# One program for self-attention and the first cross-attention of a decoder layer, with two pairs of sequences projected early

## The chip, the cores and the metric

The kernel runs on one core of a Trainium2 chip. The metric is the device time of one execution in microseconds (us). Engines: PE (TensorE) multiplies matrices into eight banks of PSUM, DVE (VectorE), ACT (ScalarE) and POOL (GpSimd) work elementwise, and SP (SyncE) issues transfers. Each engine takes its instructions in the order written and waits at semaphores.

## The reference

A decoder of two layers works on `x` of 16 sequences of 128 tokens with 256 features, in float32. The change concerns two of its six sublayers:

```python
x = x + _L0_attn_ref(_layernorm(x, axis=-1), ...)
x = x + _L0_xattn_ref(_layernorm(x, axis=-1), ctx_1024, ctx_1024, L0_xattn_W_q, L0_xattn_b_q, ...)
```

`_L0_attn_ref` is five state-space layers and then causal self-attention with 16 heads of 64, its output projection and a layer norm. `_L0_xattn_ref` is attention with 16 heads of 16 over a context of 128 tokens per sequence: Q from the normed `x`, K and V from the context, each with a bias, softmax over 128 keys, an output projection with a bias. A mixture of experts, a second self-attention, a second cross-attention and a quantized product follow; their code is unchanged.

## The kernel before

The kernel is a chain of stages. Each stage writes one program per engine inside an `nc.Block()`; all engines meet at the end of a block, and after a stage one more block clears the stage's semaphores on POOL (`clear_semaphores`).

**Self-attention** (`stage_self_attention`, L539) works in 64 ticks, `m` = 0 to 63, and ends with 8 ticks of tail, up to `LAST_TICK` = 72. The work is cut into 8 halves: 4 groups of 4 sequences, and in each two octets of heads. A tick handles 4 heads of one sequence, and two ticks make a unit (one sequence, one octet). At tick `m`, PE computes scores (L646, at even `m`), turns the probabilities of tick `m-3` (L657), multiplies those of tick `m-5` and its neighbour with V (L674) and makes the output product of tick `m-8`'s unit (L44 to L46, 12 matmuls), DVE adds the mask (L750) and takes maxima (L753), ACT takes exponentials (L707), POOL multiplies by the inverse sums (L810). The q, k and v of the next half are made by 12 "jobs" in the ticks of this half; in the last half (ticks 56 to 63) there are none. DVE adds a unit's output to `act` (octet 0) or `a_res` (octet 1) at L776, which counts up `y_added`. The layer norm follows for octet 1, and POOL adds into `x_res` (L801), which counts up `x_ready`.

**Cross-attention** (`stage_cross_attention`, L883) goes over 8 pairs of sequences for the projections and 16 sequences for attention. A pair `n` has the steps `project_k` (PE L1082), `copy_k` (four operations on DVE, L1001), `project_v` (L1091), `copy_v` (L1030), `measure` and `norm` of `x`, `turn_z` (L1099), `copy_z` (DVE L1006), `project_q` (L1107), `copy_q` (DVE L1015). They share one bank, `JOB`, so these steps of one pair, and of the next, follow one another. A sequence has `scores` (L1120, four banks `S[0..3]`, of which there is one set), `maxima` (DVE L1036, four banks), `exps` (ACT L1064, four banks of four), `invert_sums` (DVE L1040), `share_out` (POOL L962), `turn_probs` (PE L1131), `copy_probs` (ACT L1068 for banks 0, 1, 3 and DVE L921 for bank 2), `outputs` (PE L1144), `copy_out`, `project_o` (L1153) and `add`. Scores of a sequence wait for all exps of the one before. `measure_next` takes the statistics for the expert stage. The order on each engine comes from a table of places: a pair's step stands at its number plus 104 for each pair, a sequence's at its number plus 52 for each sequence, and each engine sorts its steps by place:

```python
BEAT = 52
"project_k": 91, "project_v": 117, "copy_v": 127, "measure": 14, ...
"scores": (172,), "maxima": (182, 184, 214, 200), "exps": (212, 213, 220, 218), ...
DVE_COPIES = (2,)
```

SP and ACT issue the loads at the start of the stage: the first context pair, the four weights, the biases, and then the experts' weights, one expert (1.5 MB) for each later pair (L2256). `decoder` calls the stages.

Of the kernel before, what the change touches and what calls it, by code (L numbers as in the profile page):

```python
# [12 lines left out]
F32 = mybir.dt.float32  # L13
# [4 lines left out]
ALU = mybir.AluOpType  # L18
# [520 lines left out]
def stage_self_attention(nc, ctx, io, mem):  # L539
# [15 lines left out]
    q_t = sb("q_t", [P, KW, GT])  # L555
    k_t = sb("k_t", [P, KW, GT])
    v = sb("v", [P, GS, WIDE])
# [7 lines left out]
    zb = sb("zb", [P, D])  # L565
    stats, mv, ve = mem["stats"], mem["mv"], mem["ve"]
# [43 lines left out]
    with nc.Block() as block:  # L610
        @block.tensor
        def _(pe):
            def job(half, j):
                n = half * JOBS + j
                G, octet = divmod(half, 2)
                if n >= 2:
                    pe.wait_ge((job_act, job_dve)[j % 2], n // 2)
                bank = JOB[j % 2]
                if j < 2 * OCT:
                    weights, c = (wq, wk)[j % 2], octet * OCT + j // 2  # L620
                    for k in range(KD):
                        mm = product(pe, bank[:, :], [x[:, k, c * P:(c + 1) * P] for x in weights], [x[:, k, G * GT:(G + 1) * GT] for x in ACT_T],
                                     k == 0, k == KD - 1)
                else:
                    t = G * GT + (j - 2 * OCT) * P
                    for k in range(KD):
                        mm = product(pe, bank[:, :], [x[:, k, t:t + P] for x in ACT_T],
                                     [x[:, k, octet * BANK:(octet + 1) * BANK] for x in wv], k == 0, k == KD - 1)
                mm.then_inc(job_ready, 1)

            pe.wait_ge(mem["attn_w_split"], 16)
            for j in range(JOBS):
                job(0, j)
            for m in range(LAST_TICK + 1):
                if m < TICKS and m % 2 == 0:
                    G, octet, s, _ = place(m)
                    if m % HALF_TICKS == 0:
                        jobs = (m // HALF_TICKS) * (JOBS // 2) + OCT
                        pe.wait_ge(job_act, jobs)
                        pe.wait_ge(job_dve, jobs)  # L640
                    if m >= 2:
                        pe.wait_ge(masked, m)
                    for i in range(4):
                        for par in range(2):
                            rows = slice(par * HEAD, (par + 1) * HEAD)
                            mm = pe.matmul(S[par][:, i * P:(i + 1) * P], q_t[rows, OCT * octet + i, s * P:(s + 1) * P],  # L646
                                           k_t[rows, OCT * octet + i, s * P:(s + 1) * P], start=True, stop=True,
                                           tile_position=(par * HEAD, 0))
                            if i == 3:
                                mm.then_inc(s_ready, 1)  # L650
                t = m - TURN
                if 0 <= t < TICKS:
                    pe.wait_ge(prob_ready, t + 1)
                    if t >= 2:
                        pe.wait_ge((pt_dve, pt_act)[t % 2], t // 2)
                    for i in range(4):
                        tr = pe.transpose(PT[t % 2][:, i * P:(i + 1) * P], prob[:, t % 4, i, :], ident[:, :])  # L657
                    tr.then_inc(pt_ready, 1)
                t = m - MEAN
                if 0 <= t < TICKS and t % 2 == 1:  # L660
                    G, octet, s, _ = place(t)
                    U = t // 2
                    if t % HALF_TICKS == 1:
                        jobs = (t // HALF_TICKS + 1) * (JOBS // 2)
                        pe.wait_ge(job_act, jobs)
                        pe.wait_ge(job_dve, jobs)
                    if U >= 2:
                        pe.wait_ge(y_added, U - 1)
                    pe.wait_ge(pt_dve, U + 1)
                    pe.wait_ge(pt_act, U + 1)  # L670
                    for i in range(4):
                        for par in range(2):
                            head = octet * 8 + 2 * i + par
                            mm = pe.matmul(OT(U)[par * HEAD:(par + 1) * HEAD, i * P:(i + 1) * P],  # L674
                                           v[:, s, head * HEAD:(head + 1) * HEAD], prob_t[:, (t - 1 + par) % 4, i, :],
                                           start=True, stop=True, tile_position=(0, par * HEAD))
                    mm.then_inc(ot_ready, 1)
                unit = behind(m, OUT)
                if unit:
                    U, G, octet, s = unit  # L680
                    pe.wait_ge(ot_hi, U + 1)
# [5 lines left out]
                for half, j in jobs_at(m):  # L687
                    job(half, j)
# [1630 lines left out]
```

## Time and profile before

| | us |
|---|---|
| Median of 3 runs (lowest, highest) | 1304.44 (1303.21, 1308.12) |
| Profiled execution, its own time | 1305.01 |
| Its span, first to last instruction | 1303.2 |
| PE busy / DVE busy / ACT busy / POOL busy | 1142.3 / 836.0 / 646.5 / 663.5 |
| Mean granted TensorE clock | 0.946 of full |
| First exponentials of self-attention, first scores of cross-attention, first instruction of the expert stage | 417.4, 741.3, 893.3 |

In a timeline a row gives the start, the length, the engine, the line, the operation, its output and input and how many instructions are merged; in brackets is how long the engine had been idle before and what ended that. The granted clock has two levels, 0.50 (1.2 GHz) and 1.00 (2.4 GHz), and a stretch shows their mean.

### The profile page before, as it was taken

Reading aid. Unit: us, or ns where it says so; the run is one execution under the profiler, and the core shown is the slowest. Engines: PE = TensorE matmul, PEld = TensorE weight load, DVE = VectorE, ACT = ScalarE, POOL = GpSimd, SP = SyncE. Lnnn points to the kernel's source line nnn. Section 1 sums busy time; section 2 is a strip of 40 time slices with the busy share of each in tenths; the row PEclk is TensorE's granted clock in tenths of the full one; section 3 lists DMA queues with packets and bytes.
Section 4 is the critical chain, followed back from the end, with each engine's and each line's share of the span. In section 5 each row is a group of like instructions: output and inputs, shape, how many; then the busy total and the mean of one; then the engine's idle time right before and its main releaser. Section 6 shows DMA issues by size and latency. Waiting matters only on the chain. (4 is left out here: it accounts for less than half of the span.)

```text
span 1303.2 us, 21174 instructions
## 1 busy us (share of the span) xinstructions
PE 1142.3 (88%) x6835; PEld 891.9 (68%) x6835; DVE 836.0 (64%) x1886; ACT 646.5 (50%) x1892; POOL 663.5 (51%) x706
## 2 busy tenths in 40 slices
PE   4999999999978999999975599985499999995984
PEld 3788888888866887887864477765266666664862
DVE  6888889888872666666664388873543333323795
ACT  2555555555533555555553188882122444224873
POOL 3276767767561224233344377762156656552664
PEclk9999999999998999999989599997599999997995
DMA  4002010010000000000000433204332323222001
GB/s 154 11 1 77 2 37 39 16 60 16 17 1 1 2 1 1 1 1 1 1 1 1 161 115 114 107 2 138 97 75 42 49 41 48 42 37 70 1 18 49
DMA packets 38078, 53.73 MB, mean 41 GB/s; under 512 B 8320, under 2 KB 32896, under 8 KB 36448
## 3 DMA queue, kind: packets, MB, share of 16 engines
q1 hardware_dynamic: 28672, 41.50, 9.4%
q0 software_dynamic: 8736, 10.25, 5.1%
q8 instruction: 52, 0.85, 0.3%
q10 hardware_dynamic: 576, 0.79, 0.2%
q14 instruction: 42, 0.34, 0.1%
HBM read 40.78 MB, written 11.74 MB: 40 GB/s over the span
## 5 line engine op out<-in xcount | busy, mean ns | idle before, releaser
L414 DVE SCALAR_TENSOR_TENSOR ssm_conv<-bank,conv_w,ssm_conv 128x508 f32<-128x508 f32 (+2 forms) x240 | 159.2, 727 | 9.6 <-ACT ssm_conv L350 9.6
L707 ACT ACTIVATE a_prob<-a_prob,a_neg_max 128x128 f32<-128x128 f32 x256 | 99.7, 391 | 121.3 <-DVE a_neg_max L753 121.0
L1407 PE MATMUL bank<-expert_raw,e_rows_t 128*128 x312 | 148.9, 601 | 1.2 <-ACT e_rows_t L1494 1.2
L303 PE MATMUL bank<-w_out,ssm_u 128*128 128x256 f32 x640 | 143.5, 382 | 0.0
L303 PEld LDWEIGHTS bank<-w_out,ssm_u 128*128 128x128 f32 x640 | 119.9, 190 | 17.9
L810 POOL TENSOR_TENSOR a_prob<-a_prob,a_inv 128x512 f32<-128x512 f32 x64 | 66.2, 1040 | 125.4 <-DVE a_inv L758 125.4
L1064 ACT ACTIVATE x_prob<-bank,x_neg_max 128x128 f32<-128x128 f32 x256 | 89.6, 400 | 39.1 <-DVE x_neg_max L1036 39.1
L1334 POOL DMA_INDIRECT x_rows<-e_y,e_index x39 | 62.9, 1612 | 75.8 <-ACT e_y L1522 72.0
L508 POOL TENSOR_TENSOR act_t_lo<-ssm_turned,act_t_hi 128x512 fp32r<-128x512 f32 x40 | 51.6, 1289 | 97.9 <-ACT ssm_turned L375 97.9
L1660 DVE COPY e_h_t<-bank 128x512 f32<-128x512 f32 x39 | 26.9, 691 | 105.0 <-PE bank L1416 105.0
L962 POOL TENSOR_TENSOR x_prob<-x_prob,x_inv 128x512 f32<-128x512 f32 x64 | 66.0, 1040 | 48.7 <-DVE x_inv L1040 48.7
L1407 PEld LDWEIGHTS bank<-expert_raw,e_rows_t 128*128 128x128 f32 x312 | 56.9, 193 | 42.9 <-issue 41.0
L44 PE MATMUL bank<-act_t_hi,w_in_hi 128*128 128x512 f32 x200 | 80.7, 403 | 2.5 <-PEq L66 1.7
L350 ACT ACTIVATE ssm_conv<-bank,conv_b,conv_w 128x512 f32<-128x512 f32 x80 | 62.0, 779 | 36.7 <-PE bank L46 35.6
L45 PE MATMUL bank<-act_t_lo,w_in_hi 128*128 128x512 f32 x200 | 78.9, 394 | 0.0
L46 PE MATMUL bank<-act_t_hi,w_in_lo 128*128 128x512 f32 x200 | 78.6, 393 | 0.0
L450 DVE TENSOR_SCALAR ssm_res<-ssm_res,mv,ve 128x256 f32<-128x256 f32 x80 | 71.0, 928 | 6.8 <-POOL ve L475 5.4
L1424 PE MATMUL bank<-expert_raw,e_h_t 128*128 x312 | 73.9, 380 | 0.9 <-DVE e_h_t L1660 0.9
L359 ACT ACTIVATE ssm_u<-ssm_conv 128x512 f32<-128x512 f32 x80 | 47.6, 635 | 48.5 <-DVE ssm_conv L414 48.3
L1318 POOL DMA_INDIRECT e_rows<-z_rows,e_index x39 | 38.7, 993 | 46.6 <-DVE e_index L1641 35.1
L1064 ACT ACTIVATION_READ_ACCUMULATOR x_prob<-bank,x_neg_max 128x1 f32 x256 | 61.8, 241 | 0.0
L1424 PEld LDWEIGHTS bank<-expert_raw,e_h_t 128*128 128x128 f32 x312 | 56.3, 190 | 7.6 <-issue 1.6
(328 smaller groups left out, 2997.4 us busy)
## 6 DMA issues: line engine op xcount, KB each, us to landing
expert_raw<-in_experts_laid SPq DMA_DIRECT2D x8, 1536.0 KB, 8.1
attn_raw<-in_attn_w_laid SPq DMA_DIRECT2D x4, 1024.0 KB, 7.4
w_in_raw<-in_L_attn_in_proj_w SPq DMA_DIRECT2D x5, 640.0 KB, 8.4
w_out<-in_L_attn_out_proj_w SPq DMA_DIRECT2D x5, 512.0 KB, 3.9
x_res<-in_x SPq DMA_DIRECT2D x4, 512.0 KB, 5.7
x_context<-in_ctx_t_laid SPq DMA_DIRECT2D x8, 256.0 KB, 3.6
z_rows<-cv SPq DMA_DIRECT2D x4, 512.0 KB, 2.9
x_rows<-x_res SPq DMA_DIRECT2D x4, 512.0 KB, 4.6
```

The lines of the kernel that those rows point to most:

```text
L44: pe.matmul(out, lhs[HI], rhs[HI], start=start, stop=False)
L45: pe.matmul(out, lhs[HI], rhs[LO], start=False, stop=False)
L46: return pe.matmul(out, lhs[LO], rhs[HI], start=False, stop=stop)
L303: mm = pe.matmul(UWY[h][:, s * D:(s + 1) * D], u[:, g % 2, c, t:t + P], w_out[:, c, :], start=(c == 0), stop=(c == KI - 1))
L414: op = dve.scalar_tensor_tensor(out=acc, in0=xs, scalar=conv_w[:, c, TAPS - 1 - back:TAPS - back], in1=acc, op0=ALU.mult, op1=ALU.add)
L450: dve.tensor_scalar(res[:, h, s, :], res[:, h, s, :], mv[:, i, 0:1], ve[:, i:i + 1], ALU.subtract, ALU.mult).then_inc(z_ready, 1)
L707: e = act.activation(prob[:, m % 4, i, :], prob[:, m % 4, i, :], ACT.Exp, bias=neg_max[:, m % 4, i:i + 1], accum_out=total[:, m % 4, i:i + 1])
L810: pool.tensor_tensor(prob[:, t % 4, :, :], prob[:, t % 4, :, :], inv[:, t % 4, :].unsqueeze(2).broadcast_to([P, 4, P]), ALU.mult).then_inc ...
L962: pool.tensor_tensor(prob[:, n % 2, r, :, :], prob[:, n % 2, r, :, :], inv[:, n % 2, r, :].unsqueeze(2).broadcast_to([P, 4, P]), ALU.mult) ...
L1064: e = act.activation(prob[:, n % 2, r, i, :], S[r][:, i * P:(i + 1) * P], ACT.Exp, bias=neg_max[:, n % 2, r, i:i + 1], accum_out=total[:, ...
L1407: mm = pe.matmul(bank[:, :], rows_t[:, t % 2, k, :], W[:, bass.ds(at + (column + k * FFN), FFN)], start=(k == 0), stop=(k == KD - 1))
L1424: mm = pe.matmul(Y, h_t[:, t % 2, f, :], W[:, bass.ds(at + (DOWN_AT + f * D), D)], start=(f == 0), stop=(f == KF - 1))
```

## The change

1. The two stages become functions that emit steps, and `decoder` writes one block for both. The block between them that cleared semaphores is gone. POOL clears self-attention's semaphores at the step `invert` of the last pair.
2. The projections of pairs 0 and 1 (`EARLY = 2`) are written into self-attention's ticks 56 to 64, each at the end of its tick, and use bank 2 (a bank of the jobs). From tick 72 on, cross-attention follows in each engine's program without a barrier.
3. The loads of cross-attention's weights and context start on SP once `y_added` has reached 24, those of the last weight and the experts later.
4. `copy_z`, `copy_q` and half of `copy_k` (the odd heads, now `copy_k_odd`) go from DVE to ACT; the copy of the probabilities' bank 3 goes from ACT to DVE. Every place in the table is new.
5. Cross-attention's tiles lie in memory that self-attention has finished with: weights and context over `act`, the projections' tiles over the turned activations, the experts' weights over those of self-attention.

```diff
 BY_PAIR = {
-    "project_k": 91, "project_v": 117, "copy_v": 127, "measure": 14, "invert": 0, "norm": 47, "turn_z": 135, "copy_z": 147,
+    "project_k": 75, "project_v": 115, "copy_v": 102, "measure": 0, "invert": 86, "norm": 98, "turn_z": 136, "copy_z": 127,
...
-DVE_COPIES = (2,)
+DVE_COPIES = (2, 3,)
+EARLY = 2
+EARLY_TICKS = {"clear_v": (56, 56), "selections": (57, None), "measure": (56, 59), "invert": (56, 59), "norm": (57, 60), "project_k": (57, 61), "copy_k": (57, 61),
+               "copy_k_odd": (57, 61), "project_v": (58, 62), "copy_v": (58, 62), "turn_z": (59, 63), "copy_z": (59, 63),
+               "project_q": (60, 64), "copy_q": (60, 64)}
+LEAD = {72: 0}
...
-    S, PT_BANK, JOB = psum[0:4], psum[4:6], psum[6]
+    S, PT_BANK = psum[0:4], psum[4:6]
+    job_bank = lambda n: psum[2] if n < EARLY else psum[6]
...
+        sp.wait_ge(attention["y_added"], 3 * SEQS // 2)
+        load(0, "W_k")
             load_context(0)
...
+            if G == 3:
+                sp.wait_ge(attention["x_ready"], SEQS)
+                sp.dma_start(w_o[:, :], io["L0_xattn_W_o_laid"]).then_inc(w_loaded[3], 16)
+            if G >= 3:
+                mem["load_expert"](sp, G - 3)
...
+                if n == PAIRS - 1:
+                    for handle in attention["handles"]:
+                        pool.sem_clear(handle)
...
+            elif phase == "copy_k_odd":
+                act.wait_ge(k_even, n + 1)
+                for k in range(KD):
+                    kc = act.activation(k_t[:, n % 2, 1, k, :], job_bank(n)[:, k * PT:(k + 1) * PT], ACT.Identity, bias=bk_odd[:, k:k + 1],
+                                        scale=sel[:, 1:2])
...
+            elif phase == "copy_q":
+                act.wait_ge(q_ready, n + 1)
+                    qc = act.activation(q_t[:, n % 2, k, :], job_bank(n)[:, k * PT:(k + 1) * PT], ACT.Identity, bias=bq_scaled[:, k:k + 1],
+                                        scale=XHEAD ** -0.5)
...
                 if phase == "project_k":
+                elif n == EARLY:
+                    pe.wait_ge(attention["y_added"], 2 * SEQS - 1)
...
+                @block.tensor
+                def _(pe):
+                    attention["tensor"](pe, cross["following"]("tensor"))
+                    cross["rest"]("tensor", pe)
```

DVE's order in the middle of the changed cross-attention, from the `maxima` of sequence 4 (`x_neg_max`) on. `stats` and `mv` are `measure_next`, `x_stats` is `measure`, `x_prob_t` the copies of banks 2 and 3, `x_v` is `copy_v`:

```order
750 L1061 TENSOR_REDUCE x_neg_max<-bank 128x4
751 L1017 BN_STATS stats<-x_res 128x6 x2
752 L1020 BN_AGGR mv<-stats 128x2 x2
753 L1022 TENSOR_SCALAR ve<-mv 128x2
754 L1061 TENSOR_REDUCE x_neg_max<-bank 128x4 x2
755 L1072 TENSOR_TENSOR x_res<-bank,x_res 128x256
756 L1065 RECIPROCAL x_inv<-x_total 128x4
757 L946 COPY x_prob_t<-bank 128x512 x2
758 L1065 RECIPROCAL x_inv<-x_total 128x4
759 L1055 TENSOR_TENSOR x_v<-bank,x_bv 128x16x16 x2
760 L1061 TENSOR_REDUCE x_neg_max<-bank 128x4
761 L1017 BN_STATS x_stats<-x_res 128x6 x2
```

Before, `measure_next` stood ahead of the first maximum, one copy of probabilities stood between the second and the third, and `copy_k` in place of `copy_v`.

ACT's order over two sequences of the changed cross-attention, an even one first: `x_prob` are exponentials, four to a bank, `x_z_t`, `x_q_t` and `x_k_t` the moved copies:

```order
388 L1109 ACTIVATE x_prob_t<-bank 128x512
389 L1097 ACTIVATE x_z_t<-bank 128x512
390 L1109 ACTIVATE x_prob_t<-bank 128x512
391 L1084 ACTIVATE x_prob,x_total<-bank,x_neg_max 128x128 x4
392 L1105 ACTIVATE x_q_t<-bank,x_columns 128x256 x2
393 L1084 ACTIVATE x_prob,x_total<-bank,x_neg_max 128x128 x12
394 L1109 ACTIVATE x_prob_t<-bank 128x512
395 L1092 ACTIVATE x_k_t<-bank,x_columns 128x256 x2
396 L1109 ACTIVATE x_prob_t<-bank 128x512
397 L1084 ACTIVATE x_prob,x_total<-bank,x_neg_max 128x128 x16
```

Before, the order was 16 exponentials and three copies of probabilities for each sequence, and nothing else.

DVE's order in self-attention's ticks 57 and 58 after the change. `a_` names are self-attention's, the `x_` rows are new:

```order
645 L748 TENSOR_TENSOR a_prob<-bank,causal 128x512
646 L751 TENSOR_REDUCE a_neg_max<-a_prob 128x4
647 L756 RECIPROCAL a_inv<-a_total 128x4
648 L760 COPY a_prob_t<-bank 128x512
649 L765 TENSOR_TENSOR a_o_t_lo<-bank,a_o_t_hi 128x512
650 L1027 TENSOR_REDUCE x_columns<-ident 128x2
651 L1030 TENSOR_SCALAR x_columns<-x_columns 128x2
652 L1031 TENSOR_SCALAR x_columns<-x_columns 128x2
653 L1040 TENSOR_SCALAR x_k_t<-bank,x_columns 128x256 x2
654 L748 TENSOR_TENSOR a_prob<-bank,causal 128x512
655 L751 TENSOR_REDUCE a_neg_max<-a_prob 128x4
656 L756 RECIPROCAL a_inv<-a_total 128x4
```

The mask of tick 58 (row 654) now stands behind `copy_k` of pair 0, which waits for PE's `project_k` of the same tick.

## Rows read from the trace of the kernel before

**Rows 1.** Windows: stretch; length; busy PE, PEld, DVE, ACT, POOL; clock, DMA, GB/s.

```profile
710.00:715.00 5.00, 0.90 (x8) 0.69 (x6) 2.31 (x6) 0.00 (x0) 3.67 (x6) 0.98 0.01 3
715.00:720.00 5.00, 0.00 (x0) 0.00 (x0) 0.26 (x2) 0.00 (x0) 2.67 (x5) 0.50 0.00 0
...
745.00:750.00 5.00, 3.67 (x17) 2.69 (x17) 3.95 (x13) 4.38 (x26) 2.08 (x2) 0.95 0.00 0
...
760.00:780.00 20.00, 18.50 (x183) 15.07 (x180) 17.08 (x45) 16.25 (x78) 14.25 (x15) 1.00 0.26 93
```

**Rows 2.** Timeline from the last unit of self-attention to the first maxima of cross-attention.

```profile
710.93 0.42 DVE L776 TENSOR_TENSOR a_res<-bank,act 128x256 f32<-128x256 f32 x1 [1.85 <-PE bank L46]
...
712.99 0.80 DVE L786 TENSOR_SCALAR a_z<-a_res,mv,ve 128x256 f32<-128x256 f32 x1 [0.44 <-POOL ve L817]
...
716.80 0.72 POOL L801 TENSOR_TENSOR x_res<-x_res,a_zb 128x256 f32<-128x256 f32 x1
719.69 0.66 SPq L929 DMA_DIRECT2D x_context<-in_ctx_t_laid  x1
...
723.92 3.75 PE L1082 MATMUL bank<-x_context,x_w 128*128 128x256 f32 x8 [13.02 <-DMA x_context<-in_ctx_t_laid]
...
741.30 2.09 PE L1120 MATMUL bank<-x_k_t,x_q_t 32*128 32x256 f32 x16 [1.13 <-DVE x_q_t L1015]
...
743.38 1.89 DVE L1036 TENSOR_REDUCE x_neg_max<-bank 128x4 f32<-128x512 f32 x3 [2.23 <-PE bank L1120]
```

**Rows 3.** Timeline, DVE: `y_added` reaches 24 (tick 54), and the mask of tick 63.

```profile
658.19 0.42 DVE L776 TENSOR_TENSOR a_res<-bank,act 128x256 f32<-128x256 f32 x1 [0.91 <-PE bank L46]
...
690.35 0.68 DVE L750 TENSOR_TENSOR a_prob<-bank,causal 128x512 f32<-128x512 f32 x1
```

**Rows 4.** Windows again: one microsecond in tick 58.

```profile
676.00:677.00 1.00, 1.00 (x6) 1.00 (x6) 0.00 (x0) 0.00 (x0) 0.00 (x0) 0.50 0.00 0
```

**Rows 5.** Timeline of cross-attention: sequences 11 to 14; their scores start at L1120.

```profile
841.25 0.36 ACT L1064 ACTIVATE x_prob<-bank,x_neg_max 128x128 f32<-128x128 f32 x1
...
847.06 0.72 DVE L980 BATCH_NORM_STATS2 stats<-x_res 128x6 f32<-128x256 f32 x2
847.07 1.08 ACT L1068 ACTIVATE x_prob_t<-bank 128x512 f32<-128x512 f32 x2
847.15 0.77 PEld L1120 LDWEIGHTS bank<-x_k_t,x_q_t 32*128 32x128 f32 x16 [0.35 <-issue]
...
848.35 1.28 DVE L1036 TENSOR_REDUCE x_neg_max<-bank 128x4 f32<-128x512 f32 x2
...
849.19 1.89 PE L1082 MATMUL bank<-x_context,x_w 128*128 128x256 f32 x8
...
854.04 0.37 ACT L1064 ACTIVATE x_prob<-bank,x_neg_max 128x128 f32<-128x128 f32 x1 [0.31 <-DVE x_neg_max L1036]
...
856.62 0.74 PEld L1120 LDWEIGHTS bank<-x_k_t,x_q_t 32*128 32x128 f32 x16 [0.17 <-issue]
...
864.79 0.77 PEld L1120 LDWEIGHTS bank<-x_k_t,x_q_t 32*128 32x128 f32 x16 [0.35 <-issue]
...
872.99 0.77 PEld L1120 LDWEIGHTS bank<-x_k_t,x_q_t 32*128 32x128 f32 x16 [1.21 <-issue]
```

**Rows 6.** Groups by line: operation, shapes, count, busy us, mean ns, idle before.

```profile
L921 DVE COPY x_prob_t<-bank 128x512 f32<-128x512 f32 x16 | 10.8, 678 | 0.7 <-PE bank L1131 0.7
...
L1001 DVE TENSOR_SCALAR x_k_t<-bank,x_bk,x_sel 128x256 f32<-128x256 f32 x32 | 15.2, 536 | 6.8 <-PE bank L1082 6.8
...
L1015 DVE TENSOR_SCALAR x_q_t<-bank,x_bq_scaled 128x256 f32<-128x256 f32 x16 | 7.0, 479 | 6.3 <-PE bank L1107 6.3
...
L1030 DVE TENSOR_TENSOR x_v<-bank,x_bv 128x256 f32<-128x256 f32 x16 | 6.0, 418 | 6.0 <-PE bank L1091 6.0
...
L1040 DVE RECIPROCAL x_inv<-x_total 128x4 f32<-128x4 f32 x64 | 11.0, 172 | 8.9 <-ACT x_prob L1064 8.5
...
L2027 ACT ACTIVATE l_cq_t<-bank,scaled 128x256 f32<-128x256 f32 x16 | 8.2, 560 | 2.3 <-PE bank L1888 1.9
```

More of the change, by code:

```diff
@@ new lines, in scalar, with job @@
+    def scalar(act, following):
+        def job(half, j):
+            G, octet = divmod(half, 2)
+            act.wait_ge(job_ready, half * JOBS + j + 1)
+            if j < 2 * OCT:
+                act.activation(q_t[:, octet * OCT + j // 2, :], JOB[0][:, :], ACT.Copy, scale=HEAD ** -0.5).then_inc(job_act, 1)
+            else:
+                act.activation(v[:, j - 2 * OCT, octet * BANK:(octet + 1) * BANK], JOB[0][:, :], ACT.Copy).then_inc(job_act, 1)
+        for j in range(0, JOBS, 2):
+            job(0, j)
+        for m in range(LAST_TICK + 1):
+            if m < TICKS:
+                act.wait_ge(max_ready, m + 1)
+                for i in range(4):
+                    e = act.activation(prob[:, m % 4, i, :], prob[:, m % 4, i, :], ACT.Exp,
+                                       bias=neg_max[:, m % 4, i:i + 1], accum_out=total[:, m % 4, i:i + 1])
+                e.then_inc(exp_ready, 1)
+            t = m - TURN
+            if 0 <= t < TICKS and t % 2 == 1:
+                act.wait_ge(pt_ready, t + 1)
+                act.activation(prob_t[:, t % 4, :, :], PT[1][:, :].rearrange("p (i k) -> p i k", i=4),
+                               ACT.Copy).then_inc(pt_act, 1)
+            unit = behind(m, SPLIT)
+            if unit:
+                U = unit[0]
+                act.wait_ge(ot_ready, U + 1)
+                if U > 0:
+                    act.wait_ge(y_ready, U)
+                act.activation(o_t[HI][:, :, :], OT(U).rearrange("p (i k) -> p i k", i=OCT), ACT.Copy).then_inc(ot_hi, 1)
+            for half, j in jobs_at(m):
+                if j % 2 == 0:
+                    job(half, j)
+            following(act, m)
@@ new lines, with early_turns @@
+    "add": (295,), "copy_probs": (222, 245, 253, 256), "copy_out": (281,)}
+DVE_COPIES = (2, 3,)
[4 more added lines that the diff above has]
+LEAD = {72: 0}
+def early_turns(m, phases):
+    return [(phase, n, 0) for phase in EARLY_TICKS if phase in phases for n in range(EARLY) if EARLY_TICKS[phase][n] == m]
@@ new lines, in stage_cross_attention @@
+    phases = {
+        "tensor": ("project_k", "project_v", "turn_z", "project_q", "scores", "turn_probs", "outputs", "project_o"),
+        "scalar": ("copy_k_odd", "copy_z", "copy_q", "exps", "copy_probs"),
+        "vector": ("selections", "measure", "copy_k", "copy_v", "maxima", "invert_sums", "copy_probs", "copy_out", "add", "measure_next"),
+        "gpsimd": ("clear_v", "invert", "norm", "share_out", "add_bias", "invert_next")}
+    steps = {"tensor": tensor, "scalar": scalar, "vector": vector, "gpsimd": gpsimd}
```

943 lines of the change are left out of this document (475 added, 468 removed).

## The prediction

> **What bounds the kernel now.** I read the windows first, because the change touches one seam and one stage. In the middle of cross-attention PE is busy 18.5 of 20 us, DVE 17.1 and ACT 16.3, at the full clock [rows 1]: three engines are close to full, so a step moved from one to another is not free. At the seam PE is idle from 715 to 720 and the clock stands at 0.50, one of its two levels (1.2 GHz) [rows 1]. The timeline of the seam says why. Self-attention's last output is added at 710.93, DVE's last operation ends at 713.79 (712.99 + 0.80), POOL's at 717.52 (716.80 + 0.72). Then all engines wait for the barrier and for the semaphores' clearing; the first load is issued at 719.69, PE starts at 723.92 when the context has landed, at half clock, and works through K, V and Q of pair 0 one after another, each waiting for a copy; scores start at 741.30 and the first maximum at 743.38 [rows 2]. So from DVE's last operation of one stage to its first maximum of the next there are 743.38 - 713.79 = 29.6 us in which no attention is done. Last I read the rhythm of cross-attention from the starts of the scores: 847.15, 856.62, 864.79, so an even sequence takes 9.47, an odd one 8.17 and a pair 17.64 us; the last full step, without projections, takes 8.20 (864.79 to 872.99) [rows 5].
>
> **Part 1, the seam: -29.6 us.** With projections of pairs 0 and 1 done and no barrier, DVE's first maximum of cross-attention stands right behind its last operation of self-attention. Scores of sequence 0 need only PE behind self-attention's last matmul (before 710.93) and the two early pairs. POOL is busy until 717.52, some 3.7 us longer than DVE; its first `share_out` is wanted 0.65 + 1.45 us after the maximum starts, so it comes about 1.5 us late, and what waits for it is `turn_probs`, ahead of scores 1, which are due only after all 16 exponentials (5.82 us: 841.25 to 847.07 [rows 5]). I cost that at nothing.
>
> **Part 2, the early steps in ticks 56 to 64: +7.0 us.** PE has the jobs' gaps free there, but DVE and ACT go in order, and the masks of a tick stand behind the copies of the last. DVE gets per pair: a `measure` of 1.29 (847.06 to 848.35 [rows 5]), two of `copy_k`'s operations (2 x 0.54) and two of `copy_v`'s (2 x 0.42 [rows 6]), 3.2 us, so 6.4 for both, and three tiny ones for the constants at about a reciprocal's 0.17 each, 0.5: 6.9 us. Walked tick by tick, the mask of tick 58 waits for `project_k` 0 and `copy_k` 0, that of 62 for pair 1's, and that of 63 for `copy_v` 1 behind `project_v` 1 (like `project_k` 1.9 us on PE at full clock [rows 5]) behind the output product; I get the mask of tick 63 at 697.1 instead of 690.35 [rows 3], +6.8, and 0.2 for `copy_q` 1 in the tail. The bounds: 2.5 if most falls into DVE's waits; 12.2 if all 6.9 and ACT's share too lie on the chain (per pair two `copy_k_odd` and two `copy_q` at 1.02 a pair of operations and a bank copy of 0.54 [rows 5, 6], 2.6 us). The tail's products keep their spacing. The loads go out when `y_added` is 24, at 658.6 (tick 54); from there to the mask of tick 63 are 32 us for nine ticks [rows 3], so `project_k` 0, at the end of tick 57, comes some 10 us later. The first loads took 723.92 - 719.69 = 4.2 us from issue to use [rows 2]: they are hidden with some 5 us to spare.
>
> **Part 3, the rhythm of cross-attention: +1.5 and +2.2 us.** I put the rows' durations into the new order, starting from the scores at 0. Even sequence: first maximum 1.20 to 1.85 [rows 5]; `measure_next` to 3.14; second and third maximum to 4.4; `add` 0.42; a reciprocal; two bank copies of 0.68 [rows 6]; a reciprocal; `copy_v` 0.76; the last maximum then ends near 8.0, its four exponentials (a quarter of 5.82) at 9.5, and the next scores start at 9.55. ACT had been ready for them at 6.8; DVE sets this. Before, it was the same kind of wait behind `copy_k` (0.31 at 854.04 [rows 5]) with 9.47. Odd sequence: ACT starts at 1.9, does four exponentials, then `copy_q`, then twelve: 1.9 + 5.82 + 1.02 = 8.7, and scores at 8.75, where before 8.17 passed without `copy_q` on ACT. The pair: 18.3 instead of 17.64. The gap between the last exponential and the next first one, 1.9 us, holds two bank copies of 0.54 and one of `copy_z` (0.54) or nearly `copy_k_odd` (1.02); that is why those two cost nothing, while `copy_q` stands inside the exponentials. The price of `copy_q`, 1.02 for its two operations, is two of L2027's 0.560 with scale and bias both from a tile [rows 6], overlapping by some 0.1 as the two bank copies of ACT do (1.08 together [rows 5]); the bounds are 0.96 (two of the 0.479 that DVE needed for the same copy) and 1.12 (two of 0.560).
>
> The Trainium skill (ScalarE: Activation LUTs, "What ACT_TABLE_LOAD costs") gives an activation 186 ns plus 0.833 ns per element, 93 more for each operand read from a tile, and 93 of overlap back to back. By an estimate from that page `copy_q`, which has only its bias from a tile, is two of 0.49, or 0.89 together: the sum would be 0.13 lower per pair, 0.7 over five pairs. L2027's row, with both operands from tiles, agrees with the rule (0.585 by the page, 0.560 measured).
>
> Pairs 2 to 6 take 5 x 18.3 = 91.5. Sequences 0 to 3 take 6.65 (from the first maximum), 7.9, 8.1 and 8.8, since pairs 0 and 1 are projected and `measure_next` has not begun. From first maximum to scores 14 that is 122.9; before it was 864.79 - 743.38 = 121.4: +1.5. The same walk over the old order gives 9.25 for the even sequence where the trace has 9.47, so I add 0.2 for each of eleven sequences: +2.2. Bounds: -8.5 (pair at 16.3, which is what ACT's work comes to: 11.6 of exponentials, 2.2 of copies, 0.5, 1.0, 1.0) and +8 (a pair at 19.3).
>
> **Part 4, the end and the clearing: +1.3 and +1.0 us.** Sequence 14 has `measure_next` ahead of the second maximum (0.6), and at the very end DVE makes two bank copies one after the other where ACT made one of them (0.68 [rows 6]). POOL clears self-attention's semaphores before the last pair's attention; from its last operation to the first load 2.17 us passed [rows 2], so the clears cost at most that, half hidden by a POOL that is busy 14.3 of 20 [rows 1]: +1.0, between 0 and 2.2. The experts' weights arrive later than before but all are issued by the middle of the stage: nothing.
>
> **Sum.** -29.6 + 7.0 + 1.5 + 2.2 + 1.3 + 1.0 = -16.6 us. The profiled execution took 1305.0, so 1288.4; the median of the runs lies 0.6 lower, which gives **1288**. A measurement of this kernel can tell about 0.5% (6.5 us) from no change.
>
> **Rival A, the new order fits better than my walk (1278).** If DVE's last maximum is not late, the pair comes down to ACT's sum of 16.3: 1.3 less than before instead of 0.7 more, -10 over five pairs. For it: the moves relieve DVE by about 1.3 us a pair (two of `copy_k` 0.54, one bank copy 0.68 and two of `copy_q` 0.48 go, two bank copies' worth of sequences, 1.36, come). Against it: the maxima stand behind more work in even sequences.
>
> **Rival B, the clock falls where it did not (1295).** In tick 58 PE ran at 0.50, though it was busy [rows 4]. More waits per tick for the copies can keep it low through ticks 58 to 63 and the tail. At half clock a `project_k` took 3.75 us, at full clock 1.89 [rows 2, 5]; an output product of 12 matmuls is of that length, so each unit then costs some 1.3 us more, over four to five units, with 1 to 2 for the first scores: +7. The Trainium skill (TensorE: Matmul & The Clock Gate, "The HAM clock gate") says that idleness lowers the clock to 1.2 GHz and sustained activity releases it; the seam, idle and then 0.50 until about 745 [rows 1, 2], agrees. By that rule alone an order with more waiting in the tail could lose there what it wins at the seam.
>
> **Rival C, the early steps do not come early (1292).** If the loads land after PE reaches `project_k` 0, everything of tick 58 waits behind it, and `project_v` 0 likewise; each such wait costs what the load is late, +4 for both. That is also how the change would fail to do what it says. Against it stand the 5 us above.
>
> **Rival D, ACT as the bound (1296).** If the two copies in the gap do not fit beside the probabilities' copies, a pair costs 19.5 (18.3 and the larger one's 1.02 and a little): +1.2 over six to seven pairs, some 8 us more.
>
> **Rival E, slower than before (1312).** `copy_q` waits on ACT for `project_q`, which stands on PE behind scores, `turn_z` and `copy_z`, which again is ACT's. If this ring closes late, three banks' exponentials wait behind it for PE's whole step, 1.9 us, and its copies, and the next scores with them. To be slower than before it must eat 16.6 us over six pairs, 2.8 us a pair, so a pair has to take over 21.1 us; at 22.3 the time is 1288 + 6 x 4.0 = 1312. The walk has `project_q` ready 0.4 us ahead of ACT, which speaks against it.
>
> **How the numbers follow.** Forecast 0.50, A 0.20, B 0.13, C 0.05, D 0.08, E 0.04. The forecast's own range is 1281 to 1295 (Part 2 from 2.5 to 12.2, Part 3's walk by 0.3 us a sequence). To hold 8 in 10, the range reaches into A and D: 1277 to 1298. Faster by over 0.5% means below 1297.9: the forecast, A, B, C and half of D, 0.91; within 0.5%: 0.05; slower: 0.04.
>
> **What would show it.** Right: no idle stretch of PE over 3 us between self-attention and the first maximum of cross-attention; the mask of tick 63 near 697 and the first maximum near 721; scores 18.3 us apart per pair, with ACT or DVE as the engine without gaps; DVE's busy time some 9 us lower over all, ACT's some 11 higher. Wrong: a pair at or below 17 (A); a clock of 0.50 for over 5 us in ticks 56 to 72 (B); PE waiting for a transfer at `project_k` 0 (C); a pair over 19 (D) or over 21 with ACT waiting for `project_q` (E).

## The result, and the profile after

The changed kernel takes **1298.55 us** (median of 7 runs, 1296.39 to 1303.35), the kernel before 1305.23 in its 7 runs beside it: ratio 0.995, 95% interval 0.994 to 0.997. It is faster by half a per cent, where 1.3% was forecast, and outside the range of 1277 to 1298. The profiled execution was the longest of the seven, 1303.35 us.

| | forecast | profiled execution after | missed by |
|---|---|---|---|
| First maximum, against before (743.38) | -22.6 | -20.7 | +1.9 |
| First maximum to scores 14 (before 121.4) | 125.1 | 133.9 | +8.8 |
| Scores 14 to the first instruction of the expert stage (before 28.5) | 30.8 | 31.5 | +0.7 |
| From there to the end (before 411.7) | 411.7 | 415.2 | +3.5 |
| Sum | -16.6 | -1.7 | +14.9 |

The numbers of the third column come from the timeline of the changed kernel. First its seam, in rows of SP, PE, DVE and POOL, which answer to [rows 2, 3]; L1123 is `project_k`, L748 the mask, L774 the add, L1061 the maxima, L1000 `share_out`, L1177 `turn_probs`:

```profile
657.78 0.33 SPq L949 DMA_DIRECT2D x_w<-in_L_xattn_W_k_laid  x1
...
666.33 1.89 PE L1123 MATMUL bank<-x_context,x_w 128*128 128x256 f32 x8
...
698.40 0.68 DVE L748 TENSOR_TENSOR a_prob<-bank,causal 128x512 f32<-128x512 f32 x1
...
719.89 0.42 DVE L774 TENSOR_TENSOR a_res<-bank,act 128x256 f32<-128x256 f32 x1 [1.85 <-PE bank L46]
...
721.95 0.81 DVE L784 TENSOR_SCALAR a_z<-a_res,mv,ve 128x256 f32<-128x256 f32 x1 [0.44 <-POOL ve L815]
722.67 1.87 DVE L1061 TENSOR_REDUCE x_neg_max<-bank 128x4 f32<-128x512 f32 x3
...
726.45 2.04 POOL L1000 TENSOR_TENSOR x_prob<-x_prob,x_inv 128x512 f32<-128x512 f32 x2
...
727.54 2.11 PE L1177 MATMUL bank<-ident,x_prob 128*128 128x128 f32 x8 [6.61 <-POOL x_prob L1000]
```

The loads are early (657.78, first used at 666.33, no wait), and the first maximum stands right behind DVE's last operation of self-attention, as Part 1 has it. The mask of tick 63 is at 698.40, 8.05 later than before, and the last add 8.96 later. The granted clock was 0.95 from 664 to 698 and 0.84 from 698 to 709. Then PE waits 6.61 us for POOL.

Next the starts of the scores of sequences 0, 1, 2, 4, 5 and 12 to 14, as weight loads; the second number is their length:

```profile
719.78 0.74 PEld L1164 LDWEIGHTS bank<-x_k_t,x_q_t 32*128 32x128 f32 x16
729.58 1.37 PEld L1164 LDWEIGHTS bank<-x_k_t,x_q_t 32*128 32x128 f32 x16 [0.33 <-issue]
738.32 0.77 PEld L1164 LDWEIGHTS bank<-x_k_t,x_q_t 32*128 32x128 f32 x16 [0.94 <-issue]
...
756.89 0.77 PEld L1164 LDWEIGHTS bank<-x_k_t,x_q_t 32*128 32x128 f32 x16 [0.17 <-issue]
768.41 1.37 PEld L1164 LDWEIGHTS bank<-x_k_t,x_q_t 32*128 32x128 f32 x16 [0.33 <-issue]
...
837.45 0.77 PEld L1164 LDWEIGHTS bank<-x_k_t,x_q_t 32*128 32x128 f32 x16 [0.20 <-issue]
848.07 0.77 PEld L1164 LDWEIGHTS bank<-x_k_t,x_q_t 32*128 32x128 f32 x16 [0.95 <-issue]
856.60 0.77 PEld L1164 LDWEIGHTS bank<-x_k_t,x_q_t 32*128 32x128 f32 x16 [0.79 <-issue]
```

An undisturbed pair is 837.45 to 856.60: 10.62 for the even sequence 12 and 8.53 for the odd one, 19.15 against the 18.3 of the walk and the 17.64 before [rows 5]. Two of the loads shown (and those of sequences 11 and 15) took 1.36 or 1.37 instead of 0.77: they ran at half clock, and the sequences around them are longer (sequence 4: 756.89 to 768.41, 11.52). The windows show the clock:

```profile
720.00:730.00 10.00, 3.39 (x28) 2.35 (x28) 6.56 (x19) 6.48 (x34) 8.40 (x12) 0.69 0.27 84
...
760.00:770.00 10.00, 7.12 (x70) 5.77 (x69) 6.17 (x19) 6.25 (x29) 5.57 (x7) 0.74 0.49 184
...
760.00:780.00 20.00, 17.11 (x156) 13.61 (x156) 12.51 (x34) 14.70 (x67) 11.38 (x13) 0.83 0.25 93
```

Against [rows 1], in the 20 us from 760 all four engines are less busy, DVE by 4.6 us, and the clock is 0.83 instead of 1.00. From 764 to 768, behind the waits of sequence 4, it is 0.59. No engine became the bound; they wait for each other. The timeline of sequence 12 says for what (L1084 exponentials, L946 DVE's copies of the probabilities' banks, L1192 the outputs, L1055 `copy_v`, L1164 the scores):

```profile
840.74 1.28 DVE L1061 TENSOR_REDUCE x_neg_max<-bank 128x4 f32<-128x512 f32 x2
841.45 0.37 ACT L1084 ACTIVATE x_prob<-bank,x_neg_max 128x128 f32<-128x128 f32 x1 [0.61 <-DVE x_neg_max L1061]
...
842.35 1.25 DVE L946 COPY x_prob_t<-bank 128x512 f32<-128x512 f32 x2
...
843.75 1.08 PE L1192 MATMUL bank<-x_prob_t,x_v 128*32 128x128 f32 x32 [1.46 <-DVE x_prob_t L946]
...
844.96 0.76 DVE L1055 TENSOR_TENSOR x_v<-bank,x_bv 128x256 f32<-128x256 f32 x2 [1.27 <-PE bank L1192]
845.63 0.68 DVE L1061 TENSOR_REDUCE x_neg_max<-bank 128x4 f32<-128x512 f32 x1
...
846.35 0.37 ACT L1084 ACTIVATE x_prob<-bank,x_neg_max 128x128 f32<-128x128 f32 x1 [2.00 <-DVE x_neg_max L1061]
...
848.10 1.15 PE L1164 MATMUL bank<-x_k_t,x_q_t 32*128 32x256 f32 x16 [0.74 <-ACT x_prob L1084]
```

This is the wait that the walk did not have. `x_v` has two buffers, and `copy_v` of a pair waits until the outputs of the sequence just before have read the older one (`ot_ready` at `(n-1)*PAIR`). PE's outputs wait for DVE's two bank copies, DVE's `copy_v` waits 1.27 for the outputs, the last maximum stands behind it, ACT waits 2.00 for that, and the next scores for ACT. In the old order `copy_v` stood just ahead of the odd sequence's first maximum, and its only idle time ahead of it was 6.0 us for its own projection [rows 6]. The list of waits over the ten sequences 4 to 13 of the changed kernel (us in total, times, longest):

```profile
ACT x_prob L1084 <- DVE x_neg_max L1061: 20.6, 20, 2.4
...
PE bank L1192 <- DVE x_prob_t L946: 8.5, 6, 1.5
DVE x_v L1055 <- PE bank L1192: 6.7, 5, 1.6
```

Before, from sequence 1 on, ACT's exponentials waited 2.5 us in all for a maximum. The groups by line that answer to [rows 6]:

```profile
L946 DVE COPY x_prob_t<-bank 128x512 f32<-128x512 f32 x32 | 20.4, 676 | 1.1 <-PE bank L1177 1.1
...
L1105 ACT ACTIVATE x_q_t<-bank,x_columns 128x256 f32<-128x256 f32 x16 | 6.7, 480 | 5.2 <-PE bank L1148 5.2
...
L1055 DVE TENSOR_TENSOR x_v<-bank,x_bv 128x256 f32<-128x256 f32 x16 | 6.0, 419 | 10.6 <-PE bank L1192 8.0 <-PE bank L1132 2.6
```

DVE is busy 828.3 us over all (7.7 less than before), ACT 655.3 (8.8 more): the work moved nearly as counted (9 and 11 were forecast), and the sizes held. It is the waiting that was not counted.

### The profile page after: what moved, and what is told of

It reads as the page before. It is cut to its first block and busy times, and to the rows that moved or that the text cites. A ratio compares the mean times of both kernels' runs of the same rounds, so it can differ in the third digit from the quotient of the medians.

```text
span 1301.6 us, 21160 instructions
## 1 busy us (share of the span) xinstructions
PE 1146.6 (88%) x6835; PEld 899.2 (69%) x6835; DVE 828.3 (64%) x1863; ACT 655.3 (50%) x1916; POOL 663.0 (51%) x705
## 5 line engine op out<-in xcount | busy, mean ns | idle before, releaser
L705 ACT ACTIVATE a_prob<-a_prob,a_neg_max 128x128 f32<-128x128 f32 x256 | 99.7, 391 | 122.7 <-DVE a_neg_max L751 122.7
L1084 ACT ACTIVATE x_prob<-bank,x_neg_max 128x128 f32<-128x128 f32 x256 | 90.0, 392 | 36.2 <-DVE x_neg_max L1061 36.2
L1000 POOL TENSOR_TENSOR x_prob<-x_prob,x_inv 128x512 f32<-128x512 f32 x64 | 66.0, 1039 | 52.3 <-DVE x_inv L1065 52.2
L1084 ACT ACTIVATION_READ_ACCUMULATOR x_prob<-bank,x_neg_max 128x1 f32 x256 | 59.4, 232 | 0.0
```

Of the source, the lines that this page charges most:

```text
L705: e = act.activation(prob[:, m % 4, i, :], prob[:, m % 4, i, :], ACT.Exp, bias=neg_max[:, m % 4, i:i + 1], accum_out=total[:, m % 4, i:i + 1])
L1000: pool.tensor_tensor(prob[:, n % 2, r, :, :], prob[:, n % 2, r, :, :], inv[:, n % 2, r, :].unsqueeze(2).broadcast_to([P, 4, P]), ALU.mult) ...
L1084: e = act.activation(prob[:, n % 2, r, i, :], S[r][:, i * P:(i + 1) * P], ACT.Exp, bias=neg_max[:, n % 2, r, i:i + 1], accum_out=total[:, ...
```

## The experiments

Two explanations compete for the missing time: the wait of `copy_v`, and the clock, which falls where PE has gaps. Most texts below set one against the other.

### `copy_v` behind the last maximum

```diff
-    "project_k": 75, "project_v": 115, "copy_v": 102, "measure": 0, "invert": 86, "norm": 98, "turn_z": 136, "copy_z": 127,
+    "project_k": 75, "project_v": 115, "copy_v": 104, "measure": 0, "invert": 86, "norm": 98, "turn_z": 136, "copy_z": 127,
```

> DVE's copy_v moves behind the last maximum of the same sequence, nothing else. Theory 1 (in even sequences copy_v waits for the outputs product of the sequence before, which waits for DVE's own bank copies, and the last maximum stands behind it): the even sequences that project a pair (2, 4, 6, 8, 10, 12) fall from 10.6 to about 9.6 us, ACT's wait ahead of the fourth bank's exponentials (2.0 us) to under 1.0, and the time by 5 to 7 us, to 0.990 of the kernel before. Theory 2 (the clock falling in cross-attention makes the loss): the even sequences at full clock stay at 10.6 and the time stays at 0.995.

Measured: 1294.47 us, ratio to before 0.992 (0.990 to 0.994). Even sequences fell from 10.65 (their length at full clock) to 9.85, not quite the expected 9.6, and odd ones stayed at 8.53 (822.96, 831.49, 841.34 are scores 11, 12 and 13 of this version). Only sequence 6 took 11.14. So the last maximum behind `copy_v` cost 0.8 us in every even sequence. The rest of ACT's waits stayed: 0.6 behind `measure_next`, and one for a turned bank.

### The joined program with the old order

Places, engines and `DVE_COPIES` of before; only the joining, the early pairs and the new memory stay.

```diff
-DVE_COPIES = (2, 3,)
+DVE_COPIES = (2,)
...
-        "scalar": ("copy_k_odd", "copy_z", "copy_q", "exps", "copy_probs"),
+        "scalar": ("exps", "copy_probs"),
```

> The joined program with the early pairs, but the table of places and the engines of the copies as before the change. If the seam alone is worth what the trace shows (first maximum of cross-attention 20.7 us earlier) and the new order of cross-attention cost the rest, pairs take 17.6 us again and the time falls to about 1286 (0.985). If joining the stages itself slows cross-attention (memory places, the clock after a seam without rest), pairs stay above 18.5 and the time stays above 1294.

Measured: **1286.49 us** (1285.64 to 1288.77), ratio 0.986 (0.984 to 0.989), the best version of the study and 12 us faster than the change as made (11 by the two ratios to the kernel before). Its scores 11, 12 and 13:

```profile
817.93 0.74 PEld L1179 LDWEIGHTS bank<-x_k_t,x_q_t 32*128 32x128 f32 x16 [0.17 <-issue]
826.10 0.77 PEld L1179 LDWEIGHTS bank<-x_k_t,x_q_t 32*128 32x128 f32 x16 [0.35 <-issue]
...
835.57 0.74 PEld L1179 LDWEIGHTS bank<-x_k_t,x_q_t 32*128 32x128 f32 x16 [0.17 <-issue]
```

8.17 for an odd sequence and 9.47 for an even one, exactly the rhythm of [rows 5], and the clock is 1.00 from 760 to 840. The first maximum is at 722.10, 21.3 earlier than before; 18 us of gain reach the end. Part 1 and Part 2 of the forecast stand almost as they were; the new order is what gives the gain back.

### The new order without the joining

The kernel before, with the table and the engines of the changed kernel.

```diff
-DVE_COPIES = (2,)
+DVE_COPIES = (2, 3,)
...
-            for phase, n, r in turns("exps", "copy_probs"):
+            for phase, n, r in turns("copy_k_odd", "copy_z", "copy_q", "exps", "copy_probs"):
```

> The kernel before, with two stages and the barrier, but with the new table of places and the copies on the new engines. If the new order costs what the trace of the changed kernel shows, the even sequences take 10.6 us or more and the time is 8 to 12 us above the kernel before (1.007 to 1.009). If the order is only slow beside the joined seam, the time is within 3 us of the kernel before.

Measured: 1319.69 us, ratio 1.011 (1.009 to 1.013): 15 us slower than before, where 8 to 12 were expected. In the profiled executions its first maximum comes 2.6 us later, at 745.99, and from there to scores 14 it takes 130.6 instead of 121.4. At the full clock its scores are 10.65 and 8.54 apart, so the slow pair is the order's own and needs neither the seam nor a low clock.

### PE kept busy while it waits for the first `share_out`

```diff
+KEEP_WARM = 24
...
+                if n == 0 and r == 0:
+                    pe.wait_ge(attention["y_added"], 2 * SEQS - 1)
+                    for i in range(KEEP_WARM):
+                        pe.matmul(psum[6][:, 0:PT], wk[:, 0, 0:P], wk[:, 1, :], start=True, stop=True)
```

> The changed kernel with 24 matmuls of 256 columns, whose result nobody reads, ahead of the first turn_probs, where PE waited 7 us and the granted clock then fell. Theory 2 (clock): sequence 1 falls from 8.7 to below 8.0 us and the time by 1 to 3 us. Theory 1 alone: the first sequences gain at most 1 us and the time stays within 1 us of the changed kernel's.

Measured: 1301.06 us, ratio 0.998 (0.996 to 0.999), against 0.995 for the change: no gain, where 1 to 3 us were expected. A window of this version (busy PE, PEld, DVE, ACT, POOL, then the clock) and its first scores:

```profile
750.00:840.00 90.00, 75.42 (x771) 61.38 (x770) 64.73 (x178) 74.66 (x344) 60.51 (x62) 1.00 0.32 128
```

```profile
721.52 0.74 PEld L1165 LDWEIGHTS bank<-x_k_t,x_q_t 32*128 32x128 f32 x16
734.03 0.74 PEld L1165 LDWEIGHTS bank<-x_k_t,x_q_t 32*128 32x128 f32 x16 [0.17 <-issue]
741.84 0.77 PEld L1165 LDWEIGHTS bank<-x_k_t,x_q_t 32*128 32x128 f32 x16 [1.02 <-issue]
```

With the clock held at 1.00, sequence 1 takes 7.81 instead of 8.74: its scores took 1.15 us where the changed kernel, at half clock, needed 2.09. But the added products lasted too long and made sequence 0 12.51 instead of 9.80. The pairs of sequences 6 to 11 are 10.65 + 8.54 = 19.19. That is the clean size of the new order, and the clock does not explain it. It explains the 11.17 of sequence 8, which is 10.65 here, but not all of sequence 4's 11.52: here sequence 4 takes 11.00 at 1.00. Sequence 12 is 11.16 here, with the clock at 0.58 from 845 to 849.

### Bank 3's copies back on ACT

```diff
-DVE_COPIES = (2, 3,)
+DVE_COPIES = (2,)
```

> The changed kernel with the copy of the probabilities' bank 3 back on ACT. Theory 1: the outputs wait for two bank copies of DVE; with one of them on ACT they start 0.5 to 0.7 us earlier in even sequences, copy_v and the last maximum too, so even sequences fall to 10.0 to 10.2, odd ones stay at 8.5 or rise by up to 0.5 as ACT gets a copy more: 1 to 4 us off the changed kernel's time. Rival (the bank copy is off the chain): no change within 1 us.

Measured: 1305.06 us, ratio 0.999 (0.998 to 1.000): slower than the change, where a gain was expected; a miss. Even sequences fell from 10.65 to 10.09, as Theory 1 had it, but odd ones rose from 8.53 to 10.60, at full clock. In an even sequence DVE no longer waits for the outputs, `copy_v` starts 7.0 us after the scores instead of 7.5, and ACT's 2.00 ahead of the last four exponentials is gone. What was missed is the price on ACT, here in sequence 9:

```profile
816.56 0.60 ACT L1109 ACTIVATE x_prob_t<-bank 128x512 f32<-128x512 f32 x1 [1.48 <-PE bank L1177]
```

In the new table bank 3's copy stands behind the next sequence's first four exponentials, and there ACT waits 1.48 for PE to turn it, in even and odd sequences alike, with twelve exponentials behind. On DVE the same place leaves the odd sequence at 8.53. The table and the choice of engines belong together.

### The early pairs projected after the last tick

The version with the old order, and all early steps moved to tick 72, where pair 0 is done first and pair 1 behind it.

```diff
+EARLY_TICKS = {phase: (72, 72) for phase in (
+    "clear_v", "selections", "measure", "invert", "norm", "project_k", "copy_k", "project_v", "copy_v", "turn_z", "copy_z", "project_q", "copy_q")}
```

> The joined program with the old order and engines, but both early pairs projected after tick 72, one after the other, instead of inside ticks 56 to 64. Without the early steps the mask of tick 63 is back at 690; the two pairs in series take 2 x 10 to 12 us behind self-attention's last product, partly at half clock, less what lies beside its tail. If the overlap is worth what the prediction says (two pairs for 7 to 9 us), the first maximum comes at 733 to 737 instead of 722 and the time is 1297 to 1301. If joining without a barrier brings the gain by itself, the time stays below 1291.

Measured: 1309.66 us (1303.62 to 1314.26), ratio 1.002 (1.000 to 1.004), 23 us above the version with early pairs (21 by the two ratios), and slower than the 1297 to 1301 expected: the first maximum comes at 740.25, not at 733 to 737. PE's rows at the seam:

```profile
709.00 1.89 PE L1138 MATMUL bank<-x_context,x_w 128*128 128x256 f32 x8
716.16 3.75 PE L1147 MATMUL bank<-x_w,x_context 128*128 128x256 f32 x8 [5.27 <-DVE x_k_t L1042]
...
739.11 1.15 PE L1179 MATMUL bank<-x_k_t,x_q_t 32*128 32x256 f32 x16 [1.06 <-DVE x_q_t L1055]
```

Without a barrier and with the loads long done, two pairs' projections one after another still fill 709.00 to 739.11, partly at half clock. Removing the barrier alone is worth nothing here; the seam's gain is the projecting under self-attention. The trace also prices the early steps: from the mask of tick 56 to that of tick 63 this version takes 23.30 us (663.79 to 687.09) at a clock of 1.00, the changed kernel 34.73 at 0.95. So they cost up to 11.4, of which an unknown part is the clock's. The kernel before took 25.83 for the same ticks, since its clock was at 0.82 and 0.84 from 664 to 684 where this version had 1.00.

### `measure_next` behind the third maximum

With `copy_v` behind the last maximum as in the first experiment.

```diff
-    "project_q": 159, "copy_q": 155, "add_bias": 250, "measure_next": 392, "invert_next": 446, "copy_k": 58, "copy_k_odd": 85}
+    "project_q": 159, "copy_q": 155, "add_bias": 250, "measure_next": 397, "invert_next": 446, "copy_k": 58, "copy_k_odd": 85}
```

> The order of the experiment with copy_v behind the last maximum, and measure_next behind the third maximum instead of the first. ACT's wait of 0.62 us ahead of the second bank's exponentials in even sequences should go. If it is on the path, even sequences fall from 9.85 to about 9.3 and the time to about 1291. If PE's chain (outputs, copy_v, turn_z, the turned probabilities, scores) sets the sequence, they stay at 9.85 and the time at 1294.

Measured: 1290.50 us, ratio 0.987 (0.986 to 0.989), as expected. Even sequences 9.47 (9.3 expected), odd ones 8.54.

### A third buffer for v

The order is not touched; only what `copy_v` waits for moves one pair back.

```diff
-    v = sb(low, "v", [P, 2, 2, PAIR, D])
+    v = sb(low, "v", [P, 3, 2, PAIR, D])
...
-                    dve.wait_ge(ot_ready, (n - 1) * PAIR)
+                    dve.wait_ge(ot_ready, (n - 2) * PAIR)
```

> The changed kernel with its order untouched; x_v gets a third buffer, so that copy_v waits for the outputs of two pairs ago. Theory 1 (copy_v waits for the outputs of the sequence before, because it overwrites their v): the even sequences fall from 10.65 at full clock to the 9.55 that the prediction's walk gave, and the time by 5 to 7 us, to about 1293. If copy_v's place on DVE and not its wait is the cost, they stay above 10.3.

Measured: 1292.69 us (1287.60 to 1292.93), ratio 0.987 (0.985 to 0.989). The same stretch of an even sequence as above:

```profile
832.92 1.25 DVE L946 COPY x_prob_t<-bank 128x512 f32<-128x512 f32 x2
...
834.18 0.72 DVE L1055 TENSOR_TENSOR x_v<-bank,x_bv 128x256 f32<-128x256 f32 x2
834.31 1.08 PE L1192 MATMUL bank<-x_prob_t,x_v 128*32 128x128 f32 x32 [1.48 <-DVE x_prob_t L946]
...
835.52 0.37 ACT L1084 ACTIVATE x_prob<-bank,x_neg_max 128x128 f32<-128x128 f32 x1 [0.60 <-DVE x_neg_max L1061]
```

`copy_v` no longer waits, ACT's wait fell from 2.00 to 0.60, and even sequences are 9.27 instead of 10.65 with not one instruction moved. The walk had said 9.55. This is the direct proof of the missed wait, and its price: 1.38 us in each of six sequences (2, 4, 6, 8, 10, 12), 8.3 us. The edit has a cost elsewhere: POOL clears the larger `x_v` in tick 56's early step, 2.66 us instead of 1.81, and in this profile the masks of ticks 56 to 63 span 36.68 instead of 34.73, at a clock of 0.91 instead of 0.95, and the first maximum comes at 723.80 instead of 722.67. Whether the longer clearing or the clock came first is not shown.

### A third buffer and `measure_next` later

Both edits together, with `copy_v` at its place in the change.

> The kernel after the change with both repairs of the new order: the third buffer of v (copy_v no longer waits for the outputs of the sequence just before) and measure_next behind the third maximum instead of ahead of the second. If the two costs are separate, 1.38 us (10.65 to 9.27) and 0.38 us (9.85 to 9.47) of an even sequence, the even sequence comes to 8.9 and the pair to 17.4 at the full clock, less than the old order's 17.64, and the time to 1285 to 1290. If ACT's wait behind measure_next was already hidden by something else once copy_v does not wait, the even sequence stays at 9.2 to 9.3 and the time at 1288 to 1293, as with the third buffer alone.

Measured: 1289.59 us (1285.65 to 1290.90), ratio 0.988 (0.987 to 0.990). Three of its scores:

```profile
801.20 0.77 PEld L1164 LDWEIGHTS bank<-x_k_t,x_q_t 32*128 32x128 f32 x16 [0.63 <-issue]
809.74 0.77 PEld L1164 LDWEIGHTS bank<-x_k_t,x_q_t 32*128 32x128 f32 x16 [0.18 <-issue]
818.62 0.77 PEld L1164 LDWEIGHTS bank<-x_k_t,x_q_t 32*128 32x128 f32 x16 [0.63 <-issue]
```

8.54 and 8.88: the two costs are separate, and the pair of 17.42 is a little shorter than the old order's 17.64. Yet the time is not below the old order's joined version. The first maximum comes at 724.63, there at 722.10, and its expert stage takes 43.4 us from the first transpose to the first product with expert weights, that version 41.6, which brings the next experiment in.

### PE kept busy in the gap before the expert stage

```diff
+            def _(pe):
+                for i in range(20):
+                    pe.matmul(keep["psum"][6][:, 0:P], keep["ident"][:, :], keep["ident"][:, :], start=True, stop=True)
```

In the profile of the change, transposes and router of the expert stage take longer than before (4.98 + 1.06 and 8.95 us there), though their code is the same:

```profile
889.55 6.21 PE L1428 MATMUL bank<-ident,cv 128*128 128x128 f32 x32 [8.20 <-ACT cv L1545]
895.61 11.59 PE L1436 MATMUL bank<-e_router,ck_t 128*128 128x8 f32 x64
```

> The kernel after the change, with 20 more products of 128 x 128 on PE in the block that clears the semaphores between cross-attention and the expert stage, where PE is idle for some 8 us. In the changed kernel's profile the first instruction of the expert stage comes 5.2 us earlier than before, but its first product with expert weights only 2.4 us earlier: the transposes of z took 6.21 us (before 4.98 + 1.06 with a gap) and the router's 64 products 11.59 us (before 8.95). Theory C (these 2.8 us are the clock: it rises later against the work and so covers less of it): with PE busy in the gap the clock rises earlier, transposes and router together come down by 2 us or more from 17.8, and the distance from the first transpose to the first expert product from 43.8 to under 42; the time falls by 2 to 4 us. Theory G (the gap before is what matters, or the loads that run in those 10 us are the bound): the distance stays within 0.5 us of 43.8 and so does the time.

> The joined program with the old order (the fastest version so far, 1286.5) with the same 20 products in the clearing block. There the first transpose to the first expert product took 41.6 us, with transposes and router 15.8. Theory C: the router starts further into the stretch of full clock, and the distance falls by 0 to 2 us, so 1284 to 1287. Theory G: no change.

Measured: 1300.68 us (1299.77 to 1302.00), ratio 0.997 (0.996 to 0.998), on the changed kernel; 1289.53 (1285.87 to 1295.34), ratio 0.989 (0.987 to 0.992), on the old order. The rows of the first:

```profile
882.54 6.10 PE L2210 MATMUL bank<-ident 128*128 128x128 f32 x40 [2.86 <-PEq L2332]
890.30 2.08 PE L1428 MATMUL bank<-ident,cv 128*128 128x128 f32 x16 [1.66 <-ACT cv L1545]
892.91 2.26 PE L1428 MATMUL bank<-ident,cv 128*128 128x128 f32 x16 [0.53 <-DVE cv L1625]
895.01 9.91 PE L1436 MATMUL bank<-e_router,ck_t 128*128 128x8 f32 x64
```

In this profile the stage behaves as the clock's theory says: transposes at full clock, and first transpose to first expert product 40.6 us instead of 43.8. But the products are not shown to be the reason: the version kept busy only at the start, whose code here is that of the change, took 40.9, with the router at 8.99. In the old order the products left the router at 11.86, and the distance grew from 41.6 to 42.5. What the traces do show is that transposes and router make the whole difference: they took 17.7, 15.0, 14.6, 15.8 and 16.6 us in the change, the kernel before, this version and the old order without and with the products, and the rest of the distance is 25.9 to 26.1 in all five. Of the change's extra 2.8 us, 2.6 lie in the router (11.59 against 8.95), which ran at 0.50 from 899 on; before, it was at 1.00 from 901 to 905 and at 0.50 only from 907 on. Neither kernel became faster over its runs. As a remedy it failed, and why the medians do not follow the profile stays open.

## Why the prediction was wrong

**Part 1, the seam (-29.6): right.** Without the barrier DVE goes on at once. What was read wrong in it is a side remark: the late `share_out` was costed at nothing. It did not delay the exponentials, but PE stood idle 6.61 us, where the prediction allowed 3, the clock fell, and sequence 1 took 8.74 instead of 7.81 (the version with PE kept busy). The 0.9 us are the scores at half clock, 2.09 instead of 1.15.

**Part 2, the early steps (+7.0): mis-sized, 8.9.** The chain was right (the mask of tick 63 at 698.40, not 697.1). Against a version at full clock they cost 11.4, near the upper bound of 12.2, but part of that is the changed kernel's own clock (0.95); the kernel before took 2.5 longer than that version, at 0.87. The tail added 0.9 where 0.2 was forecast, with the clock at 0.84 from 698 to 709. Nor was rival C seen: the load was issued 8.5 us before its use.

**Part 3, the rhythm (+1.5 and +2.2): the step that failed.** The walk set `copy_v` at 0.76 behind the bank copies, without what it waits for. The third buffer shows 1.38 us of waiting in each of six even sequences, 8.3 in all; with it the pair is 17.81, below the 18.3 of the walk. The odd sequence was right (8.75 walked, 8.53 measured). `copy_q` was too dear at 1.02: a pair of operations took 0.85, as the row of one shows (822.72 0.85 in the version with the third buffer). The Trainium skill (ScalarE: Activation LUTs, "What ACT_TABLE_LOAD costs") gave 0.89 by the estimate in the prediction, and the trace agrees better with it than with the row that was chosen. The allowance of 2.2 and the two dear items covered part of the missed wait: net, the pairs at full clock are 5 x (19.19 - 18.3) = 4.5 over the walk, sequence 2 is 10.04 instead of 8.1, and sequences 4 to 13 of the profiled execution are longer by another 3.8 (99.7 less 5 x 19.19), most of it where the clock was low.

**Part 4 (+1.3 and +1.0): right** to 0.7 in sum. What was missing is behind it: the expert stage took 3.5 more in the profiled execution, 2.6 of it in the router, by the clock.

**The rivals.** A (a pair at 17 or less) did not come, though 17.42 is to be had with two small edits. B named the clock as the danger, and it fell, but not mainly in ticks 58 to 72: it fell at the wait for POOL, in the ring of waits and at the expert stage. D's number, a pair of 19.5, is close to 19.19, but ACT was not the bound; it waited 20.6 us in ten sequences for maxima. E's ring through `copy_q` did not close. The true ring runs through `copy_v`, the outputs and DVE's bank copies, and no rival had it. (The chances given for a gain of over 0.5% add up to 0.92, not 0.91.)

How much of the difference the clock makes in the median, which is 4.8 us below the profiled execution, can't be told from one trace. By the medians of the two experiments that loosen `copy_v` (1292.7 and 1294.5) the missed wait is worth 4 to 6 us (by their ratios to the kernel before 4 to 11), and with `measure_next` moved as well 9.

## What to carry to other kernels

When a step is moved to another place in an engine's order, write down every semaphore that it waits for, the buffer's release above all, and where the releasing step now stands; a step that never waited can become the link of a ring, and duration alone does not show it. A change made of several parts should be tried with the parts apart: here the joining with early projections is worth 18 us and the new order takes back 12 of them. Prices of idle time on PE include the clock of what runs next.

## What the runs showed of the hardware

The clock falls in a pipeline that is busy most of the time. In the changed kernel PE was busy 68.8 of the 80 us from 760 and the clock was 0.91: it fell behind the ring's waits of sequences 4, 8 and 10. With both repairs it was busy 72.4 of 80 and the clock 1.00; before, 73.3 of 80 at 1.00. But the new order without the joining has the same ring and held 1.00 over the same 80 us with PE busy only 67.4, the version kept busy at the start likewise (75.4 of 90), and both fell to 0.6 or below for 4 us in sequence 12. So the ring's gaps can lose the clock and often do not, and what decides it is not shown. The Trainium skill (TensorE: Matmul & The Clock Gate, "The HAM clock gate") ties the lower clock to idleness, and the 6.6 us wait at the seam with 0.69 behind it agrees; that it also falls behind PE's waits of 1.0 to 1.5 us in the ring the forecast did not reckon with.

The clock also falls while PE is without a gap: the router's 64 products fill PE from 895.61 to 907.2 in the changed kernel, and three successive stretches of 2 us have the clock at 1.00, 0.72 and 0.50, the first and the last of which are these.

```profile
895.00:897.00 2.00, 2.00 (x22) 2.00 (x19) 1.21 (x2) 0.60 (x1) 0.00 (x0) 1.00 0.90 318
...
899.00:901.00 2.00, 2.00 (x11) 2.00 (x10) 0.00 (x0) 0.00 (x0) 0.00 (x0) 0.50 1.03 338
```

These are products with 8 columns. Their total is set by how much of them runs before the fall, so the same code took 8.95, 9.91 and 11.59 us in three versions.
